# Cross-attention and routed experts on one core: scatters that wait for landings, more often and in more halves

## Chip, core and metric

One NeuronCore of a Trainium2 chip runs the whole program. The metric is the device time of one execution in microseconds; several executions are timed and the median is compared. A profiler took one further execution of the kernel before: its instructions, waits, DMA queues and granted clock are read below.

## What is computed

The reference adds two blocks to x, of 4 batches x 1024 tokens x 256 features.

```
x = x + cross_attention(ctx_768, layernorm(x), mask)      # 4 heads of 64; keys: 77 context rows and the 1024 tokens
x = x + experts(layernorm(x))                             # 64 experts, 8 chosen per token, capacity 256 each

e = topk_idx.reshape(-1)
pos = jnp.take_along_axis(jnp.cumsum(oh, 0) - 1, e[:, None], 1)[:, 0]
valid = pos < CAP
buf = jnp.zeros((E, CAP + 1, h), x.dtype).at[e, pos_c].set(x[token])[:, :CAP]
y = jnp.einsum('eci,eih->ech', jax.nn.silu(g) * u, w_down)
out = jnp.zeros((n, h), jnp.float32).at[token].add(y_slots * w_slot[:, None])
```

A token's place within an expert follows from all tokens before it, and places from 256 on are dropped.

## The kernel before

Attention runs batch by batch (b = 0 to 3); a batch has two **halves** (x = 0, 1) of 512 queries, that is four tiles of 128, and each half is two blocks of nine key steps. One step makes scores (TensorE, L1281 to L1291), their exponentials (ScalarE, L1518, L1521) and the product with the values (L1308, L1313). A half's output is scaled (VectorE), projected and added to x (L1325, L1698), normalised into the array `rows` (ScalarE, L1550), turned, and the router's logits follow; VectorE then chooses eight experts for each token and works out slots and weights (kind `slot_ids`, L1790; the last operand is written at L1801).

A **scatter** (L1080) is one indirect DMA that GpSimd issues: it writes 128 rows of a tile (a token's 256 features, its number and its 64 expert weights) to the expert slots of the k-th choice, k = 0 to 7, in the DRAM array `slot_rows`. A dropped choice has an index beyond the bounds and writes nothing. A half has 4 tiles x 8 choices = 32 scatters; below they are counted n = 8q + k, 0 to 31, for tile q. Half (b, x) is named by its numbers: (3,1) is the last half of the last batch. The scatters of (2,0) and (2,1) are issued while batch 3's attention runs, those of (3,0) beside the attention of (3,1), and those of (3,1) after all attention.

When the last scatter has landed (SyncE waits on `scattered0` and `scattered1` at L1009), the expert phase begins: for 64 experts, SyncE loads an expert's rows (L1005), TensorE multiplies, and GpSimd adds the results to three DRAM planes by indirect DMA (L1155). Weights of 39 experts are loaded ahead in three groups: 16 when half (2,1)'s attention ends (L978), 6 when (3,0)'s does (L983), 17 when all attention is over (L1002).

A class `Plan` sets each engine's order from a table of costs and due times (`COST`, `SLOT`). On GpSimd it puts the scatters and the additions to the residual (`residual`, L1145: `xres` = x + bias, which VectorE's projection of the next half needs) in one fixed order; in that order the additions for the projection of (3,0) stand behind scatter 23 of (2,0), and those of (3,1) behind scatter 15 of (3,0). GpSimd executes in order: what waits there holds everything behind it.

Three rules say when a scatter may be issued, all in `scatter` (L1068): the first of a tile waits for its operands; in batches 0 to 2 a scatter waits for a certain attention step (`paced`, L542), two to a step, but three to a step in the halves of `THREE_FROM`; and in a half for which `grouped` (L549) holds, each scatter whose n is a multiple of `GROUP` (L104), other than 0, waits until all earlier scatters of the half have landed. Each scatter adds 16 to the half's semaphore when it lands, so that wait is for 16 n more than earlier batches left. Before, `grouped` holds for half (3,0) alone.

Of the kernel before, what the change touches and what calls it, by code (L numbers as in the profile page):

```python
# [18 lines left out]
B, S, D = 4, 1024, 256  # L19
# [81 lines left out]
PHASE = 2 * NKT * PR  # L101
KEY_PACE = 4
ROOM = 1
GROUP = 8  # L104
THREE_FROM = {(B - 2, 0): 107, (B - 2, 1): 119}


# [7 lines left out]
class Plan:  # L115
# [432 lines left out]

    def grouped(self, b, x):  # L549

        return (B - 2, 0) <= (b, x) < (B - 1, 1) and self.paced(b, x, 0, 0) is None

    def normed(self, at):
        b, pair = at // KEY_PAIRS, at % KEY_PAIRS
# [152 lines left out]
def program(nc, a, out, slot_rows, sums, s, ctx):  # L707
# [122 lines left out]
    plan = Plan()  # L830
# [84 lines left out]
    with ExitStack() as inner, nc.Block() as block:  # L915
# [118 lines left out]
        def _(pool):  # L1034
# [33 lines left out]
            def scatter(b, x, q, k):  # L1068
                n = part_no[(b, x, q)]
                if k == 0:  # L1070
                    pool.wait_ge(s["slots_made"], n + 1)
                    pool.wait_ge(s["rows_made"], n + 1)
                    pool.wait_ge(s["hn_made"], QT * (2 * b + x) + q + 1)
                    pool.wait_ge(s["filled"], 16 * FILLS)
                if plan.paced(b, x, q, k) and (TOPK * q + k) % (3 if (b, x) in THREE_FROM else 2) == 0:
                    pool.wait_ge(s["values_done"], plan.paced(b, x, q, k) + 1)
                before = TOPK * q + k
                if plan.grouped(b, x) and before and before % GROUP == 0:
                    pool.wait_ge(s[f"scattered{x}"], HALF_SCATTERS * b + 16 * before)
                pool.indirect_dma_start(  # L1080
                    out=slot_rows, out_offset=bass.IndirectOffsetOnAxis(ap=slot_idx[x][:, q, k:k + 1], axis=0),
                    in_=rows[x][:, q, :], in_offset=None, bounds_check=E * CAP - 1,
                    oob_is_err=False).then_inc(s[f"scattered{x}"], 16)

            for t in plan.order["pool"]:
                kind = t[0]
                if kind == "norm":
                    b, pair = t[1:]
# [11 lines left out]
                elif kind == "split":  # L1100
                    b, j = t[1:]
# [6 lines left out]
                elif kind == "norm_q":  # L1108
                    b, pair = t[1:]
# [6 lines left out]
                elif kind == "lo":  # L1116
                    b, pair = t[1:]
# [6 lines left out]
                elif kind == "ql":  # L1124
                    b, pair = t[1:]
                    at = KEY_PAIRS * b + pair
                    tiles = key_order(b)[2 * pair:2 * pair + 2]
                    x = tiles[0] // QT
                    pool.wait_ge(s["hi_made"], at + 1)
                    if b > x:  # L1130

                        wait_full(pool, ("qb", b - 1 - x, x, PR - 1, 1))
                    for i in range(2):
                        mine = slice(PR * i, PR * (i + 1))
                        ins = pool.tensor_tensor(queries(b, x)[1][:, :, tiles[i] % QT, 0:DH].rearrange(
                            "p (g e) d -> p g e d", e=2), raw_pairs(at)[:, mine],
                            quarters[:, mine, 0:4:3, :].bitcast(F32), ALU.subtract)
                    ins.then_inc(s["ql_made"], 1)
                elif kind == "residual":
                    b, x = t[1:]  # L1140
                    if (b, x) == (0, 0):
                        pool.wait_ge(s["misc_in"], 16 * 4)
                    pool.wait_ge(s["xres_loaded"], 16 * (2 * b + x + 1))
                    for j in range(QT):
                        pool.tensor_tensor(xres[:, j, :], xres[:, j, :], bo[:], ALU.add  # L1145
                                           ).then_inc(s["xres_based"], 1)
                elif kind == "scat":
                    scatter(*t[1:])
# [730 lines left out]
```

## Time and profile before

| | |
|---|---|
| median of 3 runs | 1108.94 us (1107.0 to 1112.97) |
| the profiled execution | 1109.89 us |
| its span, first to last instruction | 1108.1 us |
| busy: TensorE, VectorE, ScalarE, GpSimd | 81%, 60%, 42%, 56% of the span |
| 256 scatters (L1080) | 253.7 us of GpSimd, 991 ns each |
| 128 additions to the planes (L1155) | 84 x 1561 ns and 44 x 1564 ns |
| queues: SyncE's loads and stores, GpSimd's | 112.32 MB and 37.61 MB |

A row of the timeline gives the start, the busy time, the engine, the line and operation, and in brackets the idle time of the engine before it, with what ended it. "issue" stands for time in which the engine waited for nothing that the profile shows. A scatter's busy time is that in which GpSimd writes descriptors; the data land later.

### The profile page before, as it was taken

To read this page: it belongs to the slowest core of one execution; us is meant where nothing else is said; L and a number is where in the kernel's file an instruction comes from. 1 tells how busy PE (TensorE), PEld (TensorE's weight loads), DVE (VectorE), ACT (ScalarE), POOL (GpSimd) and SP (SyncE) were. 2 spreads that over 40 slices of the span, in tenths; PEclk is the share of its full clock that TensorE was granted. 3 is DMA by queue.
4 is the path that set the end of the run, shared out by engine and by line. 5 is a ranking of instruction groups with operands and counts; after the bars stand their busy time and mean duration, and the time that the engine had idled before them with its cause. 6 is when DMAs were issued, how large, how long until landed. Compare 5 with 4: busy or idle time off the path is not lost.

```text
span 1108.1 us, 13512 instructions
## 1 busy us (share of the span) xinstructions
PE 892.2 (81%) x3944; PEld 636.7 (57%) x3944; DVE 661.7 (60%) x1953; ACT 463.1 (42%) x931; POOL 616.9 (56%) x571
## 2 busy tenths in 40 slices
PE   2869999989999999998999987895149999888200
PEld 1446666646666656666655545784038888777100
DVE  4485638986598886597876666756514443333106
ACT  2834675743756634757443433432013333222000
POOL 4540232303785653675564673566638888888840
PEclk9979999999999999999998996987569999999755
DMA  6829801111211322210126312100739999888689
GB/s 241 303 52 386 315 1 41 39 41 63 102 68 69 124 90 64 97 57 7 65 83 228 107 35 93 34 28 18 256 126 288 314 275 164 163 156 130 71 256 392
DMA packets 85336, 150.79 MB, mean 136 GB/s; under 512 B 14089, under 2 KB 53049, under 8 KB 83215
## 3 DMA queue, kind: packets, MB, share of 16 engines
q1 hardware_dynamic: 54543, 112.32, 29.3%
q0 software_dynamic: 30720, 37.61, 17.0%
q8 instruction: 33, 0.54, 0.2%
q14 instruction: 40, 0.33, 0.1%
HBM read 69.19 MB, written 97.45 MB: 150 GB/s over the span
## 4 chain that ended last, share of the span: by engine, by line
PE 57%; DVE 14%; issue 10%; DMA 7%; POOL 6%; ACT 5%; another core or an unknown queue 1%; POOLq 0%; SPq 0%; DVEq 0%; ACTq 0%
PE ps_o L1313 17%; PE ps_u L1377 5%; PE ps_s L1289 5%; PE ps_s L1291 5%; PE ps_u L1233 4%; PE ps_u L1203 4%; POOL sum L1155 3%; DMA sum<-again,row_ids 2%; PE ps_u L1325 2%; PE ps_o L1308 2%; PE ps_o L1386 2%; DVE mp L1648 2%; DMA out_rows<-again,row_ids 2%; POOL out_rows L1155 2%; DMA again<-out_rows 2%
## 5 line engine op out<-in xcount | busy, mean ns | idle before, releaser
L1080 POOL DMA_INDIRECT slot_rows<-rows,slot_idx x256 | 253.7, 991 | 199.4 <-issue 94.4
L1648 DVE TENSOR_REDUCE mp<-ps_u 128x1 f32<-128x512 f32 x256 | 164.8, 685 | 93.0 <-PE ps_u L1233 78.7
L1518 ACT ACTIVATE probs<-ps_s 128x512 f32<-128x512 f32 x256 | 139.6, 596 | 153.7 <-PE ps_s L1291 107.9
L1155 POOL DMA_INDIRECT sum<-again,row_ids x84 | 131.1, 1561 | 26.0 <-issue 22.3
L1313 PE MATMUL ps_o<-probs,pool 128*128 128x512 f32 (+1 forms) x288 | 137.8, 601 | 4.3 <-ACT den L1539 4.3
L1377 PE MATMUL ps_u<-again 128*128 128x256 f32 x512 | 123.2, 384 | 0.0
L1313 PE MATMUL ps_o<-probs,V 128*128 128x512 f32 (+1 forms) x216 | 105.4, 610 | 5.7 <-ACT probs L1521 3.8
L1820 DVE TENSOR_SCALAR again<-ps_o,again 128x256 f32<-128x256 f32 x128 | 56.0, 479 | 77.7 <-DMA sum<-again,row_ids 50.0
L1291 PE MATMUL ps_s<-qbT,Kb 65*128 65x512 f32 (+1 forms) x252 | 102.1, 405 | 0.0
L1377 PEld LDWEIGHTS ps_u<-again 128*128 128x128 f32 x512 | 94.0, 194 | 10.6
L1155 POOL DMA_INDIRECT out_rows<-again,row_ids x44 | 68.8, 1564 | 27.0 <-DVE row_ids L1821 15.1
L1386 PE MATMUL ps_o<-again 128*128 128x256 f32 x256 | 67.4, 386 | 15.0 <-DVE again L1811 14.9
L1572 ACT ACTIVATE again<-ps_s 128x512 f32<-128x512 f32 x64 | 38.2, 597 | 97.4 <-PE ps_s L1361 87.3
L1313 PEld LDWEIGHTS ps_o<-probs,pool 128*128 128x128 f32 (+1 forms) x288 | 53.0, 192 | 45.0 <-issue 28.1
L1289 PE MATMUL ps_s<-Q,K 128*128 128x512 f32 x144 | 67.4, 468 | 6.1 <-ACT qbT L1501 5.6
L1811 DVE TENSOR_TENSOR again<-again,ps_u 128x256 f32<-128x256 f32 x64 | 26.8, 418 | 74.7 <-ACT again L1578 67.0
L1106 POOL CAST lnS<-lnT 128x256 fp32r<-128x256 f32 x24 | 10.1, 420 | 106.9 <-ACT lnT L1438 106.8
L1095 POOL TENSOR_TENSOR pool<-pool,rs_y 128x1024 f32<-128x1024 f32 (+1 forms) x20 | 33.0, 1651 | 64.7 <-DVEq L1643 64.5
L1233 PE MATMUL ps_u<-K,Q 128*128 128x512 f32 x128 | 58.7, 534 | 6.5 <-DVE mp L1648 5.6
L1203 PE MATMUL ps_u<-wqkv_hi,lnS 128*128 128x512 f32 (+1 forms) x192 | 62.4, 379 | 1.0 <-POOL lnS L1107 0.7
L1386 PEld LDWEIGHTS ps_o<-again 128*128 128x128 f32 x256 | 47.6, 190 | 26.1 <-DVE again L1811 20.2
L1313 PEld LDWEIGHTS ps_o<-probs,V 128*128 128x128 f32 (+1 forms) x216 | 40.5, 194 | 37.6 <-issue 23.3
(201 smaller groups left out, 1761.9 us busy)
## 6 DMA issues: line engine op xcount, KB each, us to landing
again<-in_wexp SPq DMA_DIRECT2D x64, 384.0 KB, 6.3
slot_rows<-rows SPq DMA_DIRECT2D x2, 10272.0 KB, 35.1
again<-slot_rows SPq DMA_DIRECT2D x64, 321.0 KB
sum<-rows SPq DMA_DIRECT2D x2, 4352.0 KB, 27.9
again<-sum SPq DMA_DIRECT2D x8, 1024.0 KB, 11.3
Kb<-K SPq DMA_DIRECT2D x16, 275.5 KB
pool<-in_x SPq DMA_DIRECT2D x4, 1024.0 KB, 5.2
xres<-in_x SPq DMA_DIRECT2D x8, 512.0 KB
```

Of the source, the lines that this page charges most:

```text
L1080: pool.indirect_dma_start(out=slot_rows, out_offset=bass.IndirectOffsetOnAxis(ap=slot_idx[x][:, q, k:k + 1], axis=0), in_=rows[x][:, q, :] ...
L1155: pool.indirect_dma_start(out=(out, *sums)[e % PLANES], out_offset=bass.IndirectOffsetOnAxis(ap=row_ids[:, e % RING, t:t + 1], axis=0), in ...
L1203: i = pe.matmul(dst, lnS[:, at % 2, rows_part, c, :], wqkv[w_part][:, c, mine], start=(c == 0 and n == 0), stop=(c == 1 and n == 2))
L1233: pe.matmul(bank((*t, i))[:, :], queries(b, x)[0][:, 2 * pr + i, tile * P:(tile + 1) * P], K[b % 2][:, 2 * pr + i, half * 512:(half + 1) * ...
L1289: pe.matmul(dst, K[b % 2][:, h, kt * P:kt * P + rk], queries(b, x)[0][:, h, :], start=True, stop=False)
L1291: pe.matmul(dst, Kb[:, h, kt * P:kt * P + rk], qbT[block_no[(b, x, pr)] % 2][:, hh, :], start=False, stop=True).then_inc(s["scores_full"], 1)
L1313: i = pe.matmul(ps_o[:, hh, :], V[b % 2][0:rk, pr, kt, DH * hh:DH * hh + P], probs[0:rk, n % NPR, hh, :], start=(kt == 0), stop=(kt == NKT ...
L1377: i = pe.matmul(ps_g[:, e % 2, which, :], w_at[e % W_BUFS][:, o:o + I], xT[e % 2][:, k, :], start=(k == 0), stop=(k == 1))
L1386: i = pe.matmul(ps_y[:, e % 2, t, :], hid[e % 2][:, t * P:(t + 1) * P], w_at[e % W_BUFS][:, 4 * I:4 * I + D], start=True, stop=True)
L1518: act.activation(probs[:, n % NPR, hh, :], ps_s[:, u % NSC, :], ACT.Exp).then_inc(s["probs_made"], 1)
L1648: v.tensor_reduce(mp[:, i, tile, half:half + 1], bank((*t, i))[:, :], AX.X, ALU.max).then_inc(s["emptied_vec"], 1)
L1820: v.tensor_scalar(y_out[r][:, t, :], ps_y[:, e % 2, t, :], xr[r][:, t, D + 1 + e:D + 2 + e], None, ALU.mult)
```

## The change

`GROUP` becomes a table by half, and `grouped` holds for the halves in it: (2,0) and (2,1) with 6, (3,0) with 4 in place of 8, and (3,1), which had no such wait, with 4. The words that go with it say of the last batch that each fourth scatter waits "but not in its last two tiles"; the code has no such exception.

```
-GROUP = 8
+GROUP = {(B - 2, 0): 6, (B - 2, 1): 6, (B - 1, 0): 4, (B - 1, 1): 4}

     def grouped(self, b, x):
-        return (B - 2, 0) <= (b, x) < (B - 1, 1) and self.paced(b, x, 0, 0) is None
+        return (b, x) in GROUP

                 before = TOPK * q + k
-                if plan.grouped(b, x) and before and before % GROUP == 0:
+                if plan.grouped(b, x) and before and before % GROUP[(b, x)] == 0:
                     pool.wait_ge(s[f"scattered{x}"], HALF_SCATTERS * b + 16 * before)
```

Instructions and their order stay as they are on all engines; only waits are added on GpSimd. In half (2,0), at scatters 4 to 8 (the end of tile 0; `values_done` counts attention steps, `scattered0` landings of half 0), GpSimd's order differs so:

```order
 L1080 DMA slot_rows<-rows,slot_idx 16384x321 x2
-L1080 DMA slot_rows<-rows,slot_idx 16384x321 [waits values_done]
+L1080 DMA slot_rows<-rows,slot_idx 16384x321 [waits scattered0,values_done]
 L1080 DMA slot_rows<-rows,slot_idx 16384x321
 L1080 DMA slot_rows<-rows,slot_idx 16384x321 [waits hn_made,filled,rows_made,slots_made]
```

Scatter 6, which already waited for a step, waits for landings as well.

In half (3,0), at tile 1 and around the additions to the residual (L1145), GpSimd's order differs so:

```order
 L1080 DMA slot_rows<-rows,slot_idx 16384x321 [waits filled,hn_made,scattered0,rows_made,slots_made]
-L1080 DMA slot_rows<-rows,slot_idx 16384x321 x7
+L1080 DMA slot_rows<-rows,slot_idx 16384x321 x3
+L1080 DMA slot_rows<-rows,slot_idx 16384x321 [waits scattered0]
+L1080 DMA slot_rows<-rows,slot_idx 16384x321 x3
 L1145 TENSOR_TENSOR xres<-xres,bo_s 128x256 [waits xres_loaded]
 L1145 TENSOR_TENSOR xres<-xres,bo_s 128x256 x3
```

The seven scatters behind the tile's first are cut in two by a new wait, and the additions stand behind both parts.

In half (3,1) the rows of before for tile 3 and those of the change for tiles 0 and 1 stand together on GpSimd:

```order
-L1080 DMA slot_rows<-rows,slot_idx 16384x321 [waits hn_made,filled,rows_made,slots_made]
-L1080 DMA slot_rows<-rows,slot_idx 16384x321 x7
+L1080 DMA slot_rows<-rows,slot_idx 16384x321 x3
+L1080 DMA slot_rows<-rows,slot_idx 16384x321 [waits scattered1]
+L1080 DMA slot_rows<-rows,slot_idx 16384x321 x3
+L1080 DMA slot_rows<-rows,slot_idx 16384x321 [waits filled,hn_made,scattered1,rows_made,slots_made]
+L1080 DMA slot_rows<-rows,slot_idx 16384x321 x3
+L1080 DMA slot_rows<-rows,slot_idx 16384x321 [waits scattered1]
```

Each tile of before waits once, for its operands; now a wait for landings stands at each fourth scatter, and tiles 2 and 3 follow with the same two kinds of wait as tile 1.

## Rows read from the trace of the kernel before

**Rows 1.** Chain of waits in order of time: start us, us, what; around the last scatter.

```profile
813.28 2.13 DMA slot_rows<-rows,slot_idx
815.46 2.77 DMA again<-slot_rows
```

**Rows 2.** Waits of SyncE's queue, 764 to 816: us in total, times, longest.

```profile
SPq L1010 <- DMA slot_rows<-rows,slot_idx: 30.7, 1, 30.7
```

**Rows 3.** Timeline of GpSimd, half (3,1): scatters 0, 16, 24, 28 and 31.

```profile
766.52 0.99 POOL L1080 DMA_INDIRECT slot_rows<-rows,slot_idx  x1 [2.15 <-issue]
...
789.94 0.98 POOL L1080 DMA_INDIRECT slot_rows<-rows,slot_idx  x1 [3.07 <-issue]
...
802.58 0.98 POOL L1080 DMA_INDIRECT slot_rows<-rows,slot_idx  x1 [2.63 <-issue]
...
809.41 0.98 POOL L1080 DMA_INDIRECT slot_rows<-rows,slot_idx  x1 [1.98 <-issue]
...
813.28 0.98 POOL L1080 DMA_INDIRECT slot_rows<-rows,slot_idx  x1 [0.30 <-issue]
```

**Rows 4.** Timeline of VectorE: first projection of (3,1); last operands of its tiles 2, 3.

```profile
740.73 0.42 DVE L1698 TENSOR_TENSOR xres<-xres,ps_u 128x256 f32<-128x256 f32 x1 [1.10 <-PE ps_u L1325]
...
788.96 0.15 DVE L1801 COPY rows<-token_id 128x1 f32<-128x1 f32 x1 [0.28 <-DVE rows L1798]
...
801.39 0.15 DVE L1801 COPY rows<-token_id 128x1 f32<-128x1 f32 x1
```

**Rows 5.** Timeline of GpSimd, half (3,0): scatter 8, the residual, scatters 16, 24, 28.

```profile
725.25 0.98 POOL L1080 DMA_INDIRECT slot_rows<-rows,slot_idx  x1 [4.29 <-DMA slot_rows<-rows,slot_idx]
...
735.27 2.88 POOL L1145 TENSOR_TENSOR xres<-xres,bo_s 128x256 f32<-128x256 f32 x4
740.47 1.00 POOL L1080 DMA_INDIRECT slot_rows<-rows,slot_idx  x1 [2.32 <-issue]
...
752.68 0.98 POOL L1080 DMA_INDIRECT slot_rows<-rows,slot_idx  x1 [2.18 <-issue]
...
759.52 0.98 POOL L1080 DMA_INDIRECT slot_rows<-rows,slot_idx  x1 [1.97 <-issue]
```

**Rows 6.** Timeline of GpSimd: (2,0) scatters 12, 18, 21; (2,1) 21; (3,0) 0.

```profile
615.75 0.98 POOL L1080 DMA_INDIRECT slot_rows<-rows,slot_idx  x1 [2.38 <-PE ps_o L1313]
...
624.29 0.98 POOL L1080 DMA_INDIRECT slot_rows<-rows,slot_idx  x1 [1.07 <-PE ps_o L1313]
...
629.36 0.98 POOL L1080 DMA_INDIRECT slot_rows<-rows,slot_idx  x1 [1.51 <-PE ps_o L1313]
...
688.97 0.98 POOL L1080 DMA_INDIRECT slot_rows<-rows,slot_idx  x1 [10.82 <-PE ps_o L1308]
...
710.95 0.98 POOL L1080 DMA_INDIRECT slot_rows<-rows,slot_idx  x1 [6.12 <-issue]
```

**Rows 7.** Timeline of SyncE's queue: xres, and weight loads of 384 KB each.

```profile
673.11 3.07 SPq L983 DMA_DIRECT2D again<-in_wexp  x6
...
718.96 0.38 SPq L994 DMA_DIRECT2D xres<-in_x  x1
...
774.43 10.29 SPq L1002 DMA_DIRECT2D again<-in_wexp  x17
```

**Rows 8.** DMA queues (packets, MB, share of 16 engines) and issues, 791 to 794.

```profile
q1 hardware_dynamic: 438, 1.20, 103.1%
...
slot_rows<-rows,slot_idx POOLq DMA_INDIRECT x3
```

**Rows 9.** The page's DMA issues: count, KB each, median us to landing.

```profile
again<-in_wexp SPq DMA_DIRECT2D x64, 384.0 KB, 6.3
```

**Rows 10.** Waits, 590 to 710: us in total, times, longest.

```profile
ACT probs L1521 <- issue: 7.2, 1, 7.2
```

**Rows 11.** Waits, 710 to 766: us in total, times, longest.

```profile
ACT probs L1518 <- remote: 4.4, 1, 4.4
...
ACT hnT L1558 <- remote: 3.5, 1, 3.5
```

## Prediction

> **What bounds the kernel now.** I read the chain of waits first, from its end. The 64 expert steps can't begin before the last scatter of the last batch has landed: it starts at 813.28, lands 2.13 us later, and SyncE then loads the first rows, at 815.46 [rows 1]. SyncE's own waits say the same: it stood 30.7 us before that load, for scatters [rows 2]. So the moment at which half (3,1)'s 32 scatters are through moves the end of the program one for one. What lies behind it (815.46 to the end) holds nothing that the change touches.
>
> Second, GpSimd's timeline of that half [rows 3]. A scatter keeps GpSimd for 0.98 us and the next starts 0.30 later: 1.29 from start to start, 28 of the 31 times between 766.52 and 813.28. Three steps are longer: 0.98 + 3.07 = 4.05 before scatter 16 (789.94), 0.98 + 2.63 = 3.61 before scatter 24 (802.58), 0.98 + 1.98 = 2.96 before scatter 28 (809.41). The first two wait for data: VectorE makes the last operand of tile 2 at 788.96 and of tile 3 at 801.39 [rows 4]. The third has no wait in the program. Its like stands at scatter 28 of half (3,0) (1.97, [rows 5]), so I take it as GpSimd's own stop after a round of descriptors, of the length of a landing. 28 x 1.29 + 4.05 + 3.61 + 2.96 = 46.7, which is the stretch.
>
> Third, how far GpSimd leads or trails elsewhere, in half (3,0) [rows 5] and in halves (2,0) and (2,1) [rows 6].
>
> **The price of one added wait.** Half (3,0) has it already, at scatters 8, 16 and 24. At 752.68 it costs 0.98 + 2.18 = 3.16 from start to start, 1.87 more than without. At 725.25, with a 512 KB load of xres beside it, 0.98 + 4.29 = 5.27. The least is GpSimd's own stop, 2.96. That is the price on quiet queues. The weights of the last 17 experts are issued from 774.43 on [rows 7], over scatters 6 and later of half (3,1). From 791 to 794 the load's queue holds all 16 DMA engines (103.1%), three scatters are issued, and not one packet of the scatters' queue starts [rows 8]. So scatter 16, issued at 789.94, lands after 794, over 4.06 after its start against 2.13 in the quiet. A wait there costs 3.16 + (4.06 - 2.13) = 5.1 or more, near the 5.27. I take 5.2, or 3.9 more than 1.29. From above I bound it by a weight load's own landing, 6.3 us [rows 9], plus the 1.03 by which 3.16 exceeds 2.13: 7.3.
>
> **Half (3,1), all of it on the path.** The words of the change leave the last two tiles out; the code doesn't, and the order shows waits at scatters 4, 8, 12, 16, 20, 24 and 28. With seven waits GpSimd is later than VectorE's operands throughout (scatter 24 would start near 813, some 12 us after the operand of 801.39), so the three long steps of before are absorbed: they give back 10.62 - 3 x 1.29 = 6.75. Scatter 28's wait takes the place of the stop. Two waits (8 and 12, at about 778 to 792) fall under the weight load: 2 x 3.9 = 7.8. Five at 1.87: 9.35. Sum 17.15 - 6.75 = **+10.4 us**.
>
> **Half (3,0): when (3,1) can begin.** New waits at 4, 12, 20 and 28. 28 falls on the stop: nothing. Scatters 4 and 12 add 3.74 before scatter 16, which idled 2.32 after the residual's additions, 2.0 beyond the usual 0.30; so +1.7. The residual, queued behind scatter 15 on GpSimd, comes 3.7 later too: VectorE's projection of (3,1) takes it, first at 740.73 [rows 4], so it loses at most some 1 us, ahead of operands that GpSimd is by then too late to use. Scatter 20 adds 1.87: 3.6. Half (3,1) idled 2.15 before 766.52, 1.85 of it slack. So its start moves by at most +1.8.
>
> **Halves (2,0) and (2,1): covered.** Each gets waits at 6, 12, 18, 24 and 30. The one at (2,0)'s 24 lies behind the residual, whose like takes 2.88 [rows 5]: nothing. That leaves seven before scatter 21 of (2,1), 7 x 1.87 = 13.1. The idle at 615.75, 624.29 and 629.36 (4.96, less 3 x 0.30) takes 4.1, and the 10.82 before 688.97 takes the rest, 9.0 of 10.5. The last two (3.7) fit into the 6.12 before 710.95 [rows 6]. If that cover goes (waits under the weight loads, as the six from 673.11 [rows 7], cost 2 more each), half (3,0) begins up to 2 us later. Who waits for these landings? Only ScalarE and VectorE, at the same half of the next batch, whose scatters begin at 710.95 at the soonest.
>
> **What may come back.** In the long runs of scatters ScalarE stands idle with no cause that the views name: 7.2 us before one masked softmax in half (2,1)'s stretch [rows 10], and 4.4 and 3.5 us put down to "remote" in half (3,0)'s [rows 11]. If shorter runs ended all this, attention would end 7.2 + 4.4 + 3.5 = 15.1 us earlier. But GpSimd couldn't follow: its slack of 10.5 + 5.8 + 4.1 = 20.4 in batch 2 less nine waits (16.8) lets half (3,0) begin 3.6 earlier at most; there it pays 5.6 and gets back 3.85 of idle, so (3,1) begins 1.8 earlier. The start therefore moves by -1.8 to +1.8; I take +0.5, as some of the cover in batch 2 will fail.
>
> **Sum.** 10.4 + 0.5 = 10.9 on the profiled execution's 1109.89 (its span and 1.79 around it): 1120.8. The median of the runs is 0.95 below that execution, so **1119.8 us**. With every wait at 2.96 and the early start: 7 x 1.67 - 6.75 - 1.8 = +3.1, or 1112. With three waits under the load at 7.3 and the late start: 4 x 1.87 + 3 x 6.0 - 6.75 + 1.8 = +20.5, or 1129.4.
>
> **Rivals.**
> *The load hardly matters.* All seven waits at 3.16: 13.1 - 6.75 + 0.5 = +6.8, 1115.7. For it: the scatters don't share the loads' queue [rows 8]. Against it: the same rows, and 725.25. The Trainium skill ("DMA: Bandwidth & Descriptors", section "Queues, rings and completion order") says that a DMA engine takes turns between its queues, a packet at a time. By that rule a scatter would wait for a packet or two and not for the load, and the sum would be this rival's; the trace's three empty microseconds disagree.
>
> *Nothing changes.* If GpSimd went on with the landing itself, a wait would be 2.13 from start to start. Scatter 24 would then start at 766.52 + 18 x 1.29 + 6 x 2.13 = 802.5, where it stands today, held by tile 3's operands, and the stop at 28 is there already: +0, 1108.9. The same would follow if the landings were mostly in before the waits. Against it: three rows of [rows 5] price the same wait at 3.16 and more.
>
> *Faster.* The idle stretches of ScalarE are the scatters' doing and go (15.1), GpSimd keeps up because its stops shrink too, and no wait meets the load: 6.4 - 15.1 = -8.7, 1100. It decides if half (3,1)'s first scatter starts before 754.6 (766.52 - 6.4 - 5.5). For it: those stretches lie in long runs of scatters and the views name no other cause. Against it: GpSimd's own floor above, 764.7.
>
> That the change isn't what its words say is settled by the order: the last two tiles do wait. Had they been left out, some 5.6 of the sum (three waits at 1.87) would be gone.
>
> **Chances and range.** Forecast 0.68, the load that hardly matters 0.12 (both slower), nothing changes 0.12, faster 0.08. 0.5% (5.5 us) is about what a measurement of this kernel tells from no change; so slower 0.80, same 0.12, faster 0.08. The forecast's own range, 1112 to 1129, holds the first rival; I put the low end at 1111 and leave out the rest.
>
> **What would show it.** In the profile after: in half (3,1) a step of 3.1 to 3.3 us (5 or more beside the load) before every fourth scatter, put down to the landing; 32 scatters taking 57 us from first to last start instead of 46.8; VectorE's last operand of tile 3 some 12 us before scatter 24; SyncE's first load of rows near 826; half (3,1) beginning within 2 us of 766.5; the expert steps' length unchanged. I am wrong if that first load comes before 821, if the added waits cost under 2.5, or if half (3,1) begins more than 5 us from 766.5.

## The result, and the profile after

The change is slower: 1122.85 us, median of 4 runs (1120.64 to 1124.64), against 1110.95 for before beside it (4 runs, 1107.0 to 1113.36). The ratio is 1.0106, 95% interval 1.0071 to 1.0141. The forecast was 1119.8 in a range of 1111 to 1129. The profiled execution took 1120.64 us (span 1118.9); the sum had said 1120.8 for it.

The total came out as the sum had it. The parts did not, so they are taken one by one. First the chain of waits of the changed kernel, in order of time (start us, us, what), at the end of the scatters:

```profile
824.87 2.13 DMA slot_rows<-rows,slot_idx
827.01 0.02 SPq L1010
827.03 0.03 issue
827.06 3.03 DMA again<-slot_rows
```

The last scatter still bounds the program, as in [rows 1]: the first load of rows is at 827.06 instead of 815.46, 11.6 us later. From there to the end of the span it is 291.8 us, before 292.6. So the whole loss lies ahead of this load.

GpSimd's timeline of half (3,1) after the change (start, busy us, engine, line, operation, idle before it and what ended it); scatters 0, 4, 8, 12, 16, 20, 24, 28 and 31:

```profile
764.17 0.98 POOL L1080 DMA_INDIRECT slot_rows<-rows,slot_idx  x1 [0.30 <-issue]
...
775.60 0.98 POOL L1080 DMA_INDIRECT slot_rows<-rows,slot_idx  x1 [6.57 <-DMA slot_rows<-rows,slot_idx]
...
786.05 0.98 POOL L1080 DMA_INDIRECT slot_rows<-rows,slot_idx  x1 [5.60 <-DMA slot_rows<-rows,slot_idx]
...
792.81 0.98 POOL L1080 DMA_INDIRECT slot_rows<-rows,slot_idx  x1 [1.92 <-DMA slot_rows<-rows,slot_idx]
...
799.66 0.98 POOL L1080 DMA_INDIRECT slot_rows<-rows,slot_idx  x1 [2.00 <-DMA slot_rows<-rows,slot_idx]
...
806.42 0.98 POOL L1080 DMA_INDIRECT slot_rows<-rows,slot_idx  x1 [1.91 <-DMA slot_rows<-rows,slot_idx]
...
813.48 0.98 POOL L1080 DMA_INDIRECT slot_rows<-rows,slot_idx  x1 [2.21 <-issue]
...
821.01 0.98 POOL L1080 DMA_INDIRECT slot_rows<-rows,slot_idx  x1 [2.68 <-issue]
...
824.87 0.98 POOL L1080 DMA_INDIRECT slot_rows<-rows,slot_idx  x1 [0.30 <-issue]
```

Against [rows 3], the three steps that waited for operands or stood at scatter 28 have become seven that wait for landings (at 24 and 28 the profile names no cause, "issue"). From start to start (0.98 and the idle time) they take 7.55, 6.58, 2.90, 2.98, 2.89, 3.19 and 3.66. With 24 steps of 1.29 that is the 60.7 us from first to last start; before it was 46.76.

SyncE's queue (the timeline, same columns) shows why it is scatters 4 and 8 that take so long:

```profile
765.54 10.34 SPq L1002 DMA_DIRECT2D again<-in_wexp  x17
827.06 3.17 SPq L1005 DMA_DIRECT2D again<-slot_rows  x7
```

The 17 weight loads, issued when attention is over, stood at 774.43 in [rows 7]. Attention now ends 8.9 us earlier, while half (3,1) begins only 2.35 us earlier (764.17 against 766.52). The loads meet the scatters from the second on instead of the seventh.

The third view is VectorE's waits (us in total, times, longest) from 764 to 789 of the changed kernel, while it works out the operands of tiles 2 and 3:

```profile
DVE sc L1718 <- ACT th L1565: 5.3, 2, 3.4
DVE wsel L1773 <- PE ps_u L1351: 0.5, 1, 0.5
```

and the same view of the kernel before, 766 to 802 (six of eleven rows; the others are 0.3 to 0.5 each):

```profile
DVE sc L1718 <- issue: 3.4, 1, 3.4
DVE sc L1718 <- ACT th L1565: 1.7, 1, 1.7
DVE wsel L1781 <- DVE rep L1774: 1.2, 1, 1.2
DVE wden L1794 <- DVE wsel L1793: 1.1, 1, 1.1
...
DVE k L1783 <- DVE wsel L1781: 0.5, 1, 0.5
DVE adj L1789 <- DVE k L1783: 0.5, 1, 0.5
...
```

Before, VectorE stood up to 1.2 us between one short operation and the next of the same chain; after, it waits only where a tile begins (L1718) and for one matmul (L1773). It has its last operand of tile 3 at 788.29, against 801.39 in [rows 4]. Of these 13.1 us, 8.7 are an earlier start (tile 2's first operation, L1718, starts at 768.21 instead of 776.88, since attention ended earlier), and 4.4 are the shorter chains. The prediction had left VectorE where it was.

### The profile page after: what moved, and what is told of

It is laid out like the page before. It is cut to its first block, busy times and chain, and to the rows that moved or that the text cites. A ratio compares the mean times of both kernels' runs of the same rounds, so it can differ in the third digit from the quotient of the medians.

```text
span 1118.9 us, 13522 instructions
## 1 busy us (share of the span) xinstructions
PE 888.3 (79%) x3944; PEld 635.5 (57%) x3944; DVE 660.2 (59%) x1953; ACT 463.1 (41%) x931; POOL 616.0 (55%) x571
## 4 chain that ended last, share of the span: by engine, by line
PE 50%; issue 14%; POOL 12%; DMA 10%; DVE 9%; ACT 4%; POOLq 1%; SPq 0%; DVEq 0%; ACTq 0%
PE ps_o L1313 15%; POOL slot_rows L1080 6%; PE ps_u L1377 5%; DMA slot_rows<-rows,slot_idx 5%; PE ps_u L1203 4%; PE ps_s L1289 4%; PE ps_s L1291 4%; PE ps_u L1233 4%; POOL sum L1155 3%; PE ps_o L1386 3%; PE ps_u L1221 2%; POOL out_rows L1155 2%; PE ps_u L1325 2%; DVE mp L1648 2%; DMA again<-out_rows 2%
## 5 line engine op out<-in xcount | busy, mean ns | idle before, releaser
L1313 PE MATMUL ps_o<-probs,V 128*128 128x512 f32 (+1 forms) x216 | 103.1, 600 | 1.7 <-issue 1.1
L1361 PE MATMUL ps_s<-ident,again 128*128 128x128 f32 x256 | 39.9, 280 | 44.7 <-DMA again<-slot_rows 44.7
```

The source lines that it names most:

```text
L1313: i = pe.matmul(ps_o[:, hh, :], V[b % 2][0:rk, pr, kt, DH * hh:DH * hh + P], probs[0:rk, n % NPR, hh, :], start=(kt == 0), stop=(kt == NKT ...
```

## The experiments

Twelve kernels were run. Each is compared with runs of the kernel before on the same chip, taken in turn with it. Before's median differed from one such group to another: 1112.83 us beside E1 to E4, 1118.03 beside E5 to E8, 1118.72 beside E9 to E11, and 1110.70 beside E12. So ratios, with their intervals, are compared, and from group to group only with care. The trace of the kernel before is of an execution of 1109.89 us; there is none from the groups where before stood at 1118.

### E1 to E4: which waits cost, and what the weight loads add

E1 takes the waits of half (3,1) out again.

```
-GROUP = {(B - 2, 0): 6, (B - 2, 1): 6, (B - 1, 0): 4, (B - 1, 1): 4}
+GROUP = {(B - 2, 0): 6, (B - 2, 1): 6, (B - 1, 0): 4}
```

> The change without its waits in half (3,1); (2,0), (2,1) with 6 and (3,0) with 4 as in the change. My theory: those waits alone make the loss. Half (3,1) begins near 764 as in the change, its scatters run 1.29 apart with the stop at scatter 28, and VectorE's operands of tiles 2 and 3 come some 9 us earlier than before, since attention ended 8.9 earlier; last scatter starts near 806, first load of rows near 808, against 815.46 before: 1103 to 1104 us, ratio near 0.993. Rival (the waits upstream carry the loss): the time stays above before, 1113 or more.

Measured: 1112.41 us, ratio 0.9991 (0.9977 to 1.0006). The loss is gone, but the gain I expected did not come. GpSimd's timeline says where it went; all rows of 756 to 818 whose idle time is not the usual 0.30 (scatter 28 of (3,0), then 16, 24 and 28 of (3,1)):

```profile
758.44 0.98 POOL L1080 DMA_INDIRECT slot_rows<-rows,slot_idx  x1 [2.67 <-issue]
...
784.57 0.98 POOL L1080 DMA_INDIRECT slot_rows<-rows,slot_idx  x1 [0.61 <-issue]
...
804.96 0.98 POOL L1080 DMA_INDIRECT slot_rows<-rows,slot_idx  x1 [10.39 <-issue]
...
811.78 0.98 POOL L1080 DMA_INDIRECT slot_rows<-rows,slot_idx  x1 [1.97 <-issue]
```

Scatter 24 stands 10.39 us for tile 3's operands, which VectorE finishes at 803.78 although attention ended 9 us earlier than before. So the waits of (3,1) do two things: they hold GpSimd up, and they let VectorE run.

E2 does what the words of the change say: no waits in the last two tiles of (3,1).

```
-                if plan.grouped(b, x) and before and before % GROUP[(b, x)] == 0:
+                if plan.grouped(b, x) and before and before % GROUP[(b, x)] == 0 and not ((b, x) == (B - 1, 1) and q >= 2):
```

> The change with its words kept: in half (3,1) the waits at 4, 8 and 12 stay, those in tiles 2 and 3 (16, 20, 24, 28) go. My theory: scatter 15 starts near 797 as in the change, the next sixteen follow 1.29 apart with one stop of 1.7 more, first load of rows near 821: 6 us later than before, 1116 to 1117 us, ratio near 1.005. Rival (the loss lies in the last two tiles, whose landings the expert phase waits for anyway): near before, 1111.

Measured: 1116.44 us, ratio 1.0036 (1.0023 to 1.0049), as expected. By the ratios the four waits of the last two tiles are 0.7% of the change's 1.06%, about 8 us. By the timelines they are less: the 32 starts span 53.03 us (763.50 to 816.53) instead of 60.70, and 1.8 of the difference lie in the two waits under the load, which took 5.90 and 6.41 here. The four waits that went then took 5.9, near the 5.6 that the prediction had given to three of them.

E3 has the waits in (3,1) alone.

```
-GROUP = {(B - 2, 0): 6, (B - 2, 1): 6, (B - 1, 0): 4, (B - 1, 1): 4}
+GROUP = {(B - 1, 0): 8, (B - 1, 1): 4}
```

> Only the waits in half (3,1); (3,0) with 8 as before and none in (2,0) and (2,1). My theory: half (3,1) begins near 766.5 as before and takes the 60.7 us of the change; first load of rows near 829: 1124 to 1126 us, slightly slower than the change. Rival (the waits upstream carry part of the loss): faster than the change, under 1120.

Measured: 1120.76 us, ratio 1.0085 (1.006 to 1.011), between the two. E1 and E3 share the change between them: half (3,1) costs 0.85%, the rest nothing that can be told. E3's four runs lie far apart, though, from 1113.86 to 1125.83.

E4 moves the 17 weight loads behind the first eight loads of rows.

```
-            wait_block(sp, (B - 1, 1, PR - 1))
-            for e in range(W_FREE[1], W_FREE[2]):
-                sp.dma_start(w_at[e], a["wexp"][e]).then_inc(s["w_early2"], 16)
...
             for e in range(RING):
                 load_rows(e)
+            wait_block(sp, (B - 1, 1, PR - 1))
+            for e in range(W_FREE[1], W_FREE[2]):
+                sp.dma_start(w_at[e], a["wexp"][e]).then_inc(s["w_early2"], 16)
```

> The change with the last 17 weight loads issued after the first eight loads of rows, so that no landing of half (3,1) meets them. My theory: the two long waits (7.55 and 6.58 from start to start) shrink to 2.9 to 3.2 each, 8 us less: first load of rows near 819, 1114 to 1115 us if the expert phase keeps its length. Rival (the load hardly matters to a landing): 1121 to 1123 as the change.

Measured: 1118.9 us, ratio 1.0052 (1.0038 to 1.0067), between the two. GpSimd's timeline of (3,1), scatters 4, 8 and 31:

```profile
770.75 0.98 POOL L1080 DMA_INDIRECT slot_rows<-rows,slot_idx  x1 [1.90 <-DMA slot_rows<-rows,slot_idx]
...
777.59 0.98 POOL L1080 DMA_INDIRECT slot_rows<-rows,slot_idx  x1 [1.99 <-DMA slot_rows<-rows,slot_idx]
...
816.48 0.98 POOL L1080 DMA_INDIRECT slot_rows<-rows,slot_idx  x1 [0.30 <-issue]
```

The same two waits take 2.88 and 2.97 us without the loads, against 7.55 and 6.58 with them: the loads add 8.3 us to the scatters. That settles the rival by which the load hardly matters. The first load of rows comes at 818.66, 8.4 earlier than in the change; but from there to the end it now takes 298.9 us instead of 291.8. The 17 weight loads now stand between the first eight loads of rows and the next ones, and TensorE, which waits for rows once in the change, waits a second time (its timeline):

```profile
853.09 1.12 PE L1361 MATMUL ps_s<-ident,again 128*128 128x128 f32 x4 [8.10 <-DMA again<-slot_rows]
```

In these two traces most of the gain is given back, 7.1 of 8.4 us; by the ratios, 1.0052 against 1.0106, about half of the loss goes.

### E5 to E8: what holds VectorE up

Two theories were open: that VectorE is slow where the weight load and the scatters meet (A), or that the run of scatters alone does it (B). E5 is E1 with the loads moved as in E4.

> No waits in half (3,1), and the 17 weight loads issued behind the first eight loads of rows. Theory A: without the waits VectorE's choices in (3,1) are held up because a weight load and an unbroken run of scatters meet; with the load gone VectorE has its last operand by about 790, scatter 24 doesn't idle, the 32 scatters run in 31 x 1.29 + 1.67 = 41.7 us from 763.6, and the first load of rows comes near 807.5, 10 earlier than without the move. The expert steps pay some 4.5 us for the late weights, as in the run that moved the loads alone: 1112.4 - 10.3 + 4.5, so 1106 to 1108. Rival B: the run of scatters alone holds VectorE up: scatter 24 idles 8 us or more again, the first load comes near 817, and the time is 1115 to 1118.

Measured: 1120.1 us, ratio 1.0015 (0.9992 to 1.0037). Theory A falls. VectorE's waits, 766 to 808, with no load beside them; of 19 rows the first five:

```profile
DVE sc L1718 <- issue: 6.5, 2, 4.6
DVE wsel L1728 <- remote: 2.5, 1, 2.5
DVE wsel L1731 <- remote: 2.5, 1, 2.5
DVE c_t L664 <- DVE c_y L666: 1.2, 1, 1.2
DVE c_nb L1712 <- DVE c_y L666: 1.2, 1, 1.2
```

Scatter 24 idles again, at 808.34, for 11.04 us.

E6 is the kernel before with the loads moved as in E4.

> The kernel before with the 17 weight loads issued behind the first eight loads of rows. Theory A (load and scatters together hold VectorE up): the gaps of VectorE at 782 to 789 go (3.9 us), scatters 16 and 24 start some 3 to 4 us earlier, the first load of rows near 811.5; the expert steps pay 4.5: within 2 us of before, 1110 to 1114. Rival B (the scatters alone): nothing is won ahead of the first load, and the time is before's plus 4.5, 1115 to 1118.

Measured: 1121.44 us, ratio 1.0034 (1.0015 to 1.0053). Tile 2's chain still takes 11.2 us without the load (12.1 with it), and the first load of rows at 813.91 is followed by 297.8 us. Theory A's gain is not there.

E7 has the waits of batch 2 alone.

```
-GROUP = {(B - 2, 0): 6, (B - 2, 1): 6, (B - 1, 0): 4, (B - 1, 1): 4}
+GROUP = {(B - 2, 0): 6, (B - 2, 1): 6, (B - 1, 0): 8}
```

> Waits at each sixth scatter in (2,0) and (2,1), (3,0) at each eighth as before, none in (3,1). Theory: the 9 us by which attention ended earlier come from the two halves of batch 2: from the 16 weight loads to the store of (3,0) the traces so far take 109.1 to 111 us with those waits, 116.6 and 120.2 without them, while from that store to the next all take 60 to 62 us, whatever (3,0) has. So here attention ends near 765 as well, the time is that of the run without waits in (3,1), 1111 to 1114, and half (3,1) can begin a few us earlier. Rival: the denser waits of (3,0) carry part of the gain: attention ends at 768 or later and the time is 1114 or more.

Measured: 1108.66 us, ratio 0.9921 (0.9895 to 0.9946): faster than before, which I had not expected. The gain of batch 2 is where it was looked for. SyncE's timeline of E7 has the 16 weight loads and the store of half (3,0) here:

```profile
591.96 10.37 SPq L978 DMA_DIRECT2D again<-in_wexp  x16
...
702.34 0.40 SPq L987 DMA_DIRECT2D out_rows<-xres  x1
```

and that of the kernel before here:

```profile
591.45 11.81 SPq L978 DMA_DIRECT2D again<-in_wexp  x16
...
711.66 0.40 SPq L987 DMA_DIRECT2D out_rows<-xres  x1
```

From the one to the other it takes 110.4 us in E7 and 120.2 before. All three traces without waits in batch 2 (before, E3, E6) take 116.6 to 121.3, all eleven with them 109.6 to 112.7. The last part of the expectation failed in the other direction: from that store to the next E7 takes 66.2 us, not 60 to 62. So attention ends at 768.95, which was the rival's mark (768 or later), though the time isn't the rival's. E9 and E10 below, which have the same waits up to there, take 68.0 and 65.8; the eleven other traces take 58.1 to 62.7. With waits in batch 2, the denser waits of (3,0) thus go with a shorter attention of (3,1); by which path, no run shows.

E8 is E1 with the loads held until VectorE has the last tile's slots.

```
             wait_block(sp, (B - 1, 1, PR - 1))
+            sp.wait_ge(s["slots_made"], part_no[(B - 1, 1, QT - 1)] + 1)
```

> No waits in half (3,1), and the 17 weight loads wait until VectorE has the slots of the last tile. Theory A: VectorE meets no load and has its last slots by about 788; the scatters run unbroken to 805, the weights move from 788 to 809 beside the last of them, whose landing takes 5 instead of 2 us: first load of rows near 810, expert steps as long as before's (292.6): 1103 to 1107, faster than before. Rival B (the run of scatters alone holds VectorE up): scatter 24 idles as without the move, the slots come near 803, the loads run to 824 and hold the first rows: 1117 or more.

Measured: 1121.04 us, ratio 1.0018 (0.9995 to 1.0042). Rival B again: VectorE is as late without a load, scatter 24 idles 11.36 us, the loads start at 806.18 and the first rows at 826.73.

### E9 to E12: one break

What E1, E5 and E8 share is a run of 28 scatters without a pause (but for 0.61 us in E1), four of (3,0) and 24 of (3,1). VectorE's first gap comes 13 to 14 us after GpSimd's last pause there, and 12 to 16 us after it in the other traces that have gaps: some ten to twelve scatters. That gave theory C: an unbroken run of more than about ten scatters slows VectorE's chain, and a pause of 3 to 5 us ends it. The traces allow less than 3: behind E6's pause of 2.40 us tile 3's chain takes 7.7 us, while E1's 0.61 us changed nothing. Whether the time or the number of scatters counts can't be told, as all runs have them 1.29 us apart.

E11 is E1 with one wait, at scatter 16 of (3,1).

```
-                if plan.grouped(b, x) and before and before % GROUP[(b, x)] == 0:
+                if (plan.grouped(b, x) and before and before % GROUP[(b, x)] == 0) or ((b, x) == (B - 1, 1) and before == 16):
```

> Half (3,1) with one wait for landings, at scatter 16, the rest as in the run without waits there. Theory C: an unbroken run of more than some 10 scatters slows VectorE's chain of short operations until the run is broken. The break before 16 (scatter 15's landing, start near 786.8 instead of 784.6) lets tile 3's chain run as in the kernel before, 7.9 us from first to last operation: its operand comes by 797, scatter 24 doesn't idle for it, the last starts near 808 and the first load of rows comes near 810 instead of 817.8. Ratio to before 0.99 to 0.994. Rival D: a break of 3 us changes nothing, VectorE is slow until GpSimd is done with tile 2: scatter 24 idles 8 us or more again, ratio 0.998 or more.

Measured: 1110.43 us, ratio 0.9913 (0.9885 to 0.9941), inside theory C's forecast. The trace bears out its mechanism and not its times. Tile 2's operands come late (789.34, and 16 starts at 790.32, not 786.8), and the first load of rows comes at 815.87, not 810. But tile 3's chain takes 7.7 us, and scatter 24 idles 2.65 us instead of 10.39, where rival D had 8 or more.

E9 is E7 with one wait, at scatter 8 of (3,1): the same line with `before == 8`.

> The run with batch 2's waits alone, and one wait in half (3,1), at scatter 8, under the weight load. Theory C: with the run cut at 8 VectorE isn't slowed, tile 2's operand comes before 782 and tile 3's before 791; scatter 8 starts near 776 instead of 771.4, but 16 doesn't idle (5.4 us before): 16 near 786.3, 24 near 796.6, 28 near 803.5, last 807.4, first load of rows near 809.5 against 812.3: ratio 0.987 to 0.992, some 0.003 below that run's 0.9921. Rival D (a single break is too short to help): tile 2's operands late as well, the wait adds its price: first load 815 or later, ratio 0.995 or more.

Measured: 1106.98 us, ratio 0.989 (0.9868 to 0.9913), inside the forecast. VectorE's waits of E9, 765 to 797, the whole answer:

```profile
DVE sc L1718 <- issue: 5.1, 2, 3.4
DVE wsel L1773 <- issue: 0.5, 1, 0.5
```

GpSimd's timeline of E9, every row of (3,1) with more than the usual idle time (scatters 0, 8 and 28), and the last:

```profile
765.32 0.98 POOL L1080 DMA_INDIRECT slot_rows<-rows,slot_idx  x1 [2.83 <-issue]
...
781.03 0.98 POOL L1080 DMA_INDIRECT slot_rows<-rows,slot_idx  x1 [5.71 <-DMA slot_rows<-rows,slot_idx]
...
808.50 0.98 POOL L1080 DMA_INDIRECT slot_rows<-rows,slot_idx  x1 [1.98 <-issue]
...
812.37 0.98 POOL L1080 DMA_INDIRECT slot_rows<-rows,slot_idx  x1 [0.30 <-issue]
```

The one wait falls under the weight load and costs 6.69 us from start to start, but 16 and 24 no longer idle, so the half takes 47.05 us, as long as before (46.76). Attention ended later here (loads at 773.23) than in E7 (768.95), which is why this one execution isn't quicker than E7's; the first load of rows comes at 814.55, against 812.28 in E7 and 809.5 in the forecast.

E10 is E9 with the weight loads held until scatters 0 to 7 have landed.

```
             wait_block(sp, (B - 1, 1, PR - 1))
+            sp.wait_ge(s["scattered1"], HALF_SCATTERS * (B - 1) + 16 * 8)
```

> As the run with one wait at scatter 8, and the 17 weight loads wait for the landing of scatters 0 to 7 too. The wait at 8 is then quiet: scatter 8 starts near 773.2, 16 near 783.5, 24 near 793.9, 28 near 800.7, the last 804.6; the loads move from 773 to 794, out of the way of the last landing: first load of rows near 807, ratio 0.984 to 0.989. Rival: load and scatters together slow VectorE after six scatters, as in the run without waits, 24 idles for tile 3's operands: first load 811 or later, ratio 0.991 or more.

Measured: 1108.36 us, ratio 0.99 (0.9877 to 0.9924), between the forecast and its rival, and not told apart from E9. The wait at 8 became quiet (1.99 us idle), but with it shorter the run from scatter 8 begins earlier against VectorE: tile 3's chain starts 11.0 us into it (7.0 in E9) and takes 13.8 us, and scatter 24 idles 5.67 us. What the wait saves comes back one tile later.

E12 is E1 with the wait at scatter 8, that is E9 with (3,0) at each fourth.

> Half (3,0) at each fourth scatter, as in the change, and one wait in half (3,1), at scatter 8. Theory C: with VectorE unhindered the waits of (3,0) no longer matter, since what they did was to set how long a run of scatters VectorE met. Half (3,1) starts near 763, scatter 8 comes some 6 us after 7 (under the load), VectorE has tile 2's operand before 784 and tile 3's before 797, 16 and 24 don't idle, and the 32 starts span 46 to 48 us: the same as with each eighth in (3,0), ratio 0.986 to 0.992. Rival: the denser waits of (3,0) cost by themselves the 0.7% that lie between the two runs without a wait in (3,1) (0.9991 and 0.9921): ratio 0.995 or more.

Measured: 1107.76 us, ratio 0.9976 (0.9959 to 0.9994): the rival's number, with the theory's trace (of an execution of 1103.05 us). Half (3,1) spans 46.67 us (760.98 to 807.65), and 16 and 24 don't idle. But before was at 1110.70 here and at 1118.72 beside E9, a difference larger than the one in question, while E9 and E12 lie 0.8 us apart in time. What (3,0)'s denser waits cost by themselves stays open. Of all kernels run, E9 has the best ratio to before, 0.989, though its interval overlaps those of E7, E10 and E11.

How large these gains are stays open too. From the 16 weight loads (L978) to the end of the span, the traces take 516.7 us before, 513.7 in E7, 514.1 in E9, 515.4 in E10, 514.4 in E11 and 509.7 in E12: 1 to 3 us less in E7 and E9 to E11, whose medians lie 8 to 12 us below that of before beside them. No trace shows where before spends the other us when its median is 1118.

The times of VectorE's chain, from L1718 to the last operand (L1801), read from the timelines:

| kernel | tile 2, us | tile 3, us |
|---|---|---|
| change; E2; E3; E4 | 7.5; 7.8; 7.6; 7.6 | 7.8; 7.7; 7.7; 7.7 |
| before; E6 | 12.1; 11.2 | 7.7; 7.7 |
| E1; E5; E8 (28 scatters unbroken) | 14.7; 13.7; 13.6 | 12.4; 13.1; 12.1 |
| E7; E11 (a pause at 16) | 14.2; 18.9 | 7.7; 7.7 |
| E9; E12 (a wait at 8) | 7.6; 9.6 | 8.2; 8.3 |
| E10 (a wait at 8, earlier) | 7.6 | 13.8 |

A chain is long where the run of scatters beside it is long, with and without a load (E5, E6 and E8 have none beside it).

## Why the prediction was right, and where its steps were not

- **What bounds the kernel** held: the last scatter of (3,1) sets the end one for one, and the expert steps kept their length.
- **Half (3,1), quiet waits.** Five waits with the stop were priced at 5 x 3.16 = 15.8 us; they took 2.90 + 2.98 + 2.89 + 3.19 + 3.66 = 15.6. Right.
- **Half (3,1), waits under the load.** Two at 5.2 were expected, at scatters 8 and 12; there were two, at 4 and 8, and they took 7.55 and 6.58, 3.7 us more together. The first is above the upper bound of 7.3. This is the term that was too small. The rule that went with the rival (the Trainium skill, "DMA: Bandwidth & Descriptors", section "Queues, rings and completion order": a DMA engine takes turns between queues by packet) was read there as a packet or two that cost next to nothing, so that the wait would be 3.16 beside the load too. The trace has 7.55 beside it and, in E4, 2.88 without it; these rows refute that reading. They don't refute the rule itself, since no view here shows how much of the load one packet in its sense holds.
- **The start of (3,1)** was put at +0.5, in -1.8 to +1.8; it was -2.35, below the range. Attention did end earlier, by 8.9 us, and the "remote" waits of [rows 11] are gone. As the prediction had it, GpSimd could not follow: (3,1) begins right behind (3,0), with 0.30 idle.
- **The residual of (3,1)** was to cost VectorE's projection at most some 1 us. In the change VectorE stands 7.55 us for it, behind GpSimd's new waits (row below). The term was mis-sized without harm: the projection still starts at 735.62, earlier than the 740.73 of [rows 4], and (3,1) begins when GpSimd is through with (3,0).

```profile
735.62 0.42 DVE L1698 TENSOR_TENSOR xres<-xres,ps_u 128x256 f32<-128x256 f32 x1 [7.55 <-POOL xres L1145]
```

- **Batch 2, covered**: right and too cautious. Half (3,0) begins at 709.20 against 710.95 in [rows 6]. E7 (0.9921) shows that these waits alone are a gain, if not of what size.
- **VectorE** was the step that was wrong in kind. "VectorE's last operand of tile 3 some 12 us before scatter 24" took its start and its speed as given; it was 25 us, 8.7 of the difference by the earlier start and 4.4 by the speed. In the change this is worth nothing, since GpSimd is too late to use it. It decides as soon as the waits are thinned out: E1 shows it by its absence, E9 by its presence.
- **The sum** came out as 11.6 us ahead of the first load, against 10.9: the loads' +3.7 and the start's -2.85 nearly cancel. Part of the agreement is luck.
- **Words and code**: the exception that the words name costs time, 5.9 us by the timelines and 0.7% by the ratios (E2), though not all of the loss.
- The rival "nothing changes" fell with the quiet waits: 2.9 us and more from start to start, not 2.13.
- The rival "faster" fell at its own point: (3,1) did not start before 754.6. Its mechanism, long runs of scatters that slow other engines, is nevertheless what E7 to E12 use.

## What to carry to other kernels

Here a wait for landings counted in three places: on the engine that waits, on an engine whose input is queued behind the wait (the residual), and on the engine that works beside the run it breaks. Count the first two from the timeline, and look in the waits of the others for gaps between dependent short operations: if they come only late in long runs, one break in the right place (E9) may buy what seven (the change) cannot. Where a wait for small transfers falls under a bulk load, price it by what it costs under that load; but moving the load away is worth only what the load doesn't then take from the next stage.

## What the hardware did that I had not expected

VectorE's chain for a tile took 12 to 14 us instead of 7.5 to 8 beside an unbroken run of indirect DMAs on GpSimd, with no weight load about (E5, E8). The operations themselves did not get longer: L1793 takes 218 ns in E5's long chains and 216 in the change's short ones, and the 40 operations of tile 2's chain are busy 7.5 us in E5 and 7.2 in the change. Only the gaps grow, from one operation to the next that needs it. Side by side, the end of tile 2 in E5's timeline of VectorE:

```profile
781.49 0.17 DVE L1790 SCALAR_TENSOR_TENSOR slot_idx<-k,adj 128x8 uint32<-128x8 f32 x1 [0.54 <-DVE adj L1789]
...
782.90 0.17 DVE L1796 RECIPROCAL wden<-wden 128x1 f32<-128x1 f32 x1 [0.67 <-issue]
783.61 0.23 DVE L1798 SCALAR_TENSOR_TENSOR rows<-wsel,wden 128x64 f32<-128x64 f32 x1 [0.54 <-DVE wden L1796]
784.32 0.15 DVE L1801 COPY rows<-token_id 128x1 f32<-128x1 f32 x1 [0.48 <-DVE rows L1798]
```

and in the change's:

```profile
774.50 0.17 DVE L1790 SCALAR_TENSOR_TENSOR slot_idx<-k,adj 128x8 uint32<-128x8 f32 x1
...
775.28 0.16 DVE L1796 RECIPROCAL wden<-wden 128x1 f32<-128x1 f32 x1
775.48 0.22 DVE L1798 SCALAR_TENSOR_TENSOR rows<-wsel,wden 128x64 f32<-128x64 f32 x1
775.74 0.15 DVE L1801 COPY rows<-token_id 128x1 f32<-128x1 f32 x1
```

From the first of these operations to the last it is 2.83 us and 1.24 us. The Trainium skill ("GPSIMD Engine Reference", section "Specifications") says that GpSimd shares its SBUF interfaces with VectorE, with contention for VectorE's operations in a 2-port mode or with two SBUF inputs. If that were all, the gaps would be looked for beside any scatter; here they begin only 12 to 16 us into a run, and E9 has none beside scatters that keep GpSimd just as long (0.98 us each). They also outlast the run: GpSimd's last scatter before the pause in E5 is written by 797.30, and a gap that lies wholly behind it ends here (VectorE's timeline):

```profile
800.52 0.17 DVE L1731 TENSOR_TENSOR wsel<-wsel 128x16 f32<-128x16 f32 x1 [2.45 <-remote]
```

Nor do the traces point to the loading of instructions: between 758 and 812 each has one packet of an instruction queue, which falls into tile 3's chain in the change (784.95, a short chain) as in E5 (798.82, a long one). So the runs show when the slowing begins and that a pause ends it, and not by which path it comes. The attention of (3,0), beside the scatters of batch 2, takes 109.6 to 112.7 us with waits there and 116.6 to 121.3 without; the same cause would fit, but no run isolates it.
